# Projections from mixed token tiles, keys scaled on GpSimd, and a new spacing of the background steps beside a recurrent scan

## What is computed

```python
x = _layernorm(x + _L0_attn_ref(...))   # gated linear recurrence
x = _layernorm(x + _L0_xattn_ref(...))  # LSTM with attention in every step
x = _layernorm(x + _L0_ffn_ref(...))    # 8 experts, 2 a token: the FIRST mixture
x = _layernorm(x + _L1_attn_ref(...))   # the scan below
x = _layernorm(x + _L1_xattn_ref(...))  # cross attention
x = _layernorm(x + _L1_ffn_ref(...))    # 4 experts and a shared one: the SECOND mixture
```

```python
shifted = jnp.concatenate([zeros_like(h[:, :1]), h[:, :-1]], axis=1)
delta = shifted - h
xr = h + delta * x_r          # and xw, xk, xv, xa with x_w, x_k, x_v, x_a
r = xr @ W_r
log_w = -softplus(-(tanh(xw @ w_lora_a) @ w_lora_b + w_bias)) - 0.5
k = xk @ W_k
v = xv @ W_v
a = sigmoid(xa @ a_lora_a @ a_lora_b + a_bias)
g = sigmoid(r @ g_lora_a) @ g_lora_b + g_bias
kk = (k * k_k).reshape(Bn, Tn, H, D)
kk = kk / maximum(norm(kk, axis=-1, keepdims=True), 1e-12)
k = k * (1.0 + (a - 1.0) * k_a)
def step(S, xs):              # 512 steps, one after the other
    r_t, w_t, k_t, v_t, a_t, b_t = xs          # a = -kk, b = kk * a
    sa = einsum('bhij,bhj->bhi', S, a_t)
    S = S * exp(w_t)[:, :, None, :] + sa[..., None] * b_t[:, :, None, :] + v_t[..., None] * k_t[:, :, None, :]
    return S, einsum('bhij,bhj->bhi', S, r_t)
```

## Time and profile before

| | |
|---|---|
| time, median of 3 runs | 6065.13 us (6060.26 to 6067.42) |
| the profiled execution's own time | 6056.11 us |
| its span in the trace | 6054.3 us |
| busy in the span: PE, DVE, ACT, POOL | 5506.3, 3606.7, 2103.8, 317.7 us |
| mean granted TensorE clock | 0.973 of full speed |
| ahead of the tail phase's first scan step | 4342.3 us |
| the 512 scan steps | 4342.3 to 5785.6 us |
| what is left after them | 5785.6 to 6054.3 us |

### The profile page before, as it was taken

How to read it: one execution, slowest core, us unless ns; L and a number is a source line. 1 busy time by engine, 2 the same in 40 slices (tenths; PEclk the granted TensorE clock), 3 DMA queues, 4 the chain that set the end, 5 groups by cost and what they waited for, 6 DMA issues and landing times. The chain is left out here.

```text
span 6054.3 us, 385300 instructions
## 1 busy us (share of the span) xinstructions
PE 5506.3 (91%) x171736; PEld 3879.1 (64%) x171736; DVE 3606.7 (60%) x16290; ACT 2103.8 (35%) x8003; POOL 317.7 (5%) x779
## 2 busy tenths in 40 slices
PE   6899999999999999999999999999888879887989
PEld 2577777777777777777777777777644444444433
DVE  4355555555555555555555555555487898888831
ACT  3144444444444444444444444444222122223221
POOL 0000000000000000000000000000011111111000
PEclk8999999999999999999999999999899899899989
DMA  1100000000000000000000000000211101011111
GB/s 69 57 2 2 2 2 2 2 2 2 2 2 2 2 2 2 2 2 2 2 2 2 2 2 2 2 2 17 81 58 40 40 28 47 31 45 33 47 38 54
DMA packets 45135, 111.64 MB, mean 18 GB/s; under 512 B 8160, under 2 KB 10208, under 8 KB 44528
## 3 DMA queue, kind: packets, MB, share of 16 engines
q1 hardware_dynamic: 43600, 109.39, 5.6%
q10 hardware_dynamic: 1440, 1.06, 0.1%
HBM read 99.90 MB, written 10.52 MB: 18 GB/s over the span
## 5 line engine op out<-in xcount | busy, mean ns | idle before, releaser
L711 PE MATMUL lstm_part_ps<-lstm_keys,lstm_hid 128*4 128x128 f32 x32768 | 1024.1, 273 | 205.5 <-DVE lstm_hid L880 205.5
L727 PE MATMUL lstm_ctx_ps<-lstm_values,lstm_alpha 128*4 128x128 f32 (+1 forms) x49152 | 1051.4, 237 | 0.2 <-issue 0.2
L711 PEld LDWEIGHTS lstm_part_ps<-lstm_keys,lstm_hid 128*4 128x4 f32 x32768 | 771.3, 86 | 427.2 <-DVE lstm_hid L880 413.6
L727 PEld LDWEIGHTS lstm_ctx_ps<-lstm_values,lstm_alpha 128*4 128x4 f32 x49152 | 904.8, 86 | 90.7 <-issue 0.4
L909 DVE TENSOR_REDUCE lstm_neg_max<-lstm_part_ps 128x1 f32<-128x128 f32 x1024 | 299.1, 292 | 678.8 <-PE lstm_part_ps L711 678.8
L842 ACT ACTIVATE lstm_expo<-lstm_part_ps,lstm_neg_max 128x128 f32<-128x128 f32 x1024 | 376.4, 368 | 862.2 <-DVE lstm_neg_max L909 862.2
L670 PE MATMUL lstm_half_ps<-lstm_w_hid,lstm_hid 128*13 128x96 f32 x16384 | 596.0, 246 | 0.0
L862 DVE STREAM_TRANSPOSE lstm_gates<-lstm_half_ps 128x96 f32<-128x96 f32 x1026 | 290.1, 283 | 396.1 <-PE lstm_half_ps L670 372.0
L670 PE MATMUL lstm_half_ps<-lstm_w_attn,lstm_attn 128*13 128x96 f32 x16448 | 526.0, 248 | 0.0
L670 PEld LDWEIGHTS lstm_half_ps<-lstm_w_attn,lstm_attn 128*13 128x13 f32 x16448 | 300.5, 93 | 154.6 <-ACT lstm_attn L855 106.7
L1944 ACT ACTIVATE mix_gated<-mix_gate_ps 115x512 f32<-115x512 f32 (+2 forms) x200 | 112.6, 563 | 820.0 <-PE mix_gate_ps L1674 819.9
(11 more groups left out here) (336 smaller groups left out, 8593.0 us busy)
## 6 DMA issues: line engine op xcount, KB each, us to landing
mix_ring<-in_sm_chunks SPq DMA_DIRECT2D x120, 358.0 KB, 2.9
mix_ring<-in_mix_chunks SPq DMA_DIRECT2D x80, 384.0 KB, 3.0
lstm_xg<-xg_rows SPq DMA_DIRECT2D x514, 16.0 KB
xg_rows<-lstm_xg_tile SPq DMA_DIRECT2D x16, 512.0 KB, 2.6
ctxT<-in_ctxT SPq DMA_DIRECT2D x1, 2048.0 KB, 14.6
out_xT<-xT SPq DMA_DIRECT2D x4, 512.0 KB, 3.8
xT<-in_xT SPq DMA_DIRECT2D x1, 1536.0 KB, 9.8
lstm_w_x<-in_lstm_w_x SPq DMA_DIRECT2D x1, 1024.0 KB, 10.8
```

The lines of the kernel that those rows point to most:

```text
L711: mm = pe.matmul(part_rows(score_ps[part], b), hid[:, k, lo:lo + SPACE], keys[:, k, b * SRC + c * P:b * SRC + (c + 1) * P], start=(n == 0 ...
L727: mm = pe.matmul(part_rows(ctx_ps[n], b), alpha[:, b, c, SPACE - 1 - c:2 * SPACE - 1 - c], values[:, b * SC + c, ctx_cols[n]], start=(c == ...
```

## The change

Five things change, all in the tail phase.

1. The weights stay as they are loaded. For each tile GpSimd makes the difference of the two token tiles (`step_x`, 1 instruction, scan step 0), and VectorE makes five mixed tiles of it, one for each of r, w, k, v, a (`mix_x`, 10 SCALAR_TENSOR_TENSOR of 128x128, scan step 1). TensorE's `sums` has 2 products instead of 4. `project_columns` moves from step 0 to step 2 and waits for `mix_x`; ScalarE's `project_products` moves from step 1 to step 3.
2. The keys scaled by k_k are no longer a projection: ScalarE copies k, GpSimd multiplies it (`scale_keys`, step 5), and ScalarE squares that (`square_keys`, step 7).
3. `CHAIN_SLOTS = 1`: the hops of the norms and of the cross attention are 1 step apart instead of 2.
4. `CHUNK_SLOTS` is (3, 3) for the SECOND mixture; it stays (2, 3) for FIRST.
5. The weight preparation on VectorE ahead of the scan goes (16 instructions).

```diff
-CHUNK_SLOTS = (2, 3)
+CHAIN_SLOTS = 1
+CHUNK_SLOTS = {MIXTURE0: (2, 3), MIXTURE1: (3, 3)}
...
-                yield from attention(q, SLOTS)
+                yield from attention(q, CHAIN_SLOTS)
                 yield from mixture(SECOND, q, SLOTS)
...
-                for part in (OWN, LAST):
-                    for k in range(KC):
-                        mm = pe.matmul(out, lhs(part, k), rhs(part, k), start=(part == OWN and k == 0),
-                                       stop=(part == LAST and k == KC - 1))
+                for k in range(KC):
+                    mm = pe.matmul(out, lhs(k), rhs(k), start=(k == 0), stop=(k == KC - 1))
...
+            def mixed(name):
+                return lambda k: x_mix[:, MIXES.index(name), k, :]
...
             def project_columns(m):
-                pe.wait_ge(x_copied, m + 1)
+                pe.wait_ge(x_mixed, m + 1)
...
-                for n, name in enumerate(("k", "kk")):
-                    mm = sums(k_ps[:, n, :], x, lambda part, k: w[name][:, part, k, :])
-                mm.then_inc(keys_ready, 1)
+                sums(k_ps[:, 0, :], mixed("k"), lambda k: w["k"][:, k, :]).then_inc(keys_ready, 1)
...
-                if has_next and t == 0:
+                if has_next and t == 2:
                     project_columns(c + 1)
...
                 pe.wait_ge(added, added_by_mixture(x, i) + 1)
                 ln.mean(pe, lambda k: token_block(x, i)[:, k, :], g.mean_mat[:, :], width)
-                yield from pause(slots)
+                yield from pause(CHAIN_SLOTS)
                 ln.variance(pe, norm_after_mixture(x, i), g.mean_mat[:, :], width)
-                yield from pause(slots)
+                yield from pause(CHAIN_SLOTS)
                 ln.spread(pe, norm_after_mixture(x, i), g.spread, width)
-                yield from pause(slots)
+                yield from pause(CHAIN_SLOTS + 1)
...
             def keep_keys(m):
                 act.wait_ge(keys_ready, m + 1)
-                act.activation(kk_sq[:, :], k_ps[:, 1, :], ACT.Square).then_inc(kk_sq_ready, 1)
-                act.copy(k[:, :], k_ps[:, 0, :])
-                act.copy(kk[:, :], k_ps[:, 1, :]).then_inc(kk_ready, 1)
+                act.copy(k[:, :], k_ps[:, 0, :]).then_inc(k_copied, 1)
+
+            def square_keys(m):
+                act.wait_ge(kk_ready, m + 1)
+                act.activation(kk_sq[:, :], kk[:, :], ACT.Square).then_inc(kk_sq_ready, 1)
...
+            def step_x(m):
+                pool.wait_ge(x_copied, m + 1)
+                pool.tensor_tensor(x_step[:, :, :], x_in[:, LAST, :, :], x_in[:, OWN, :, :], ALU.subtract).then_inc(x_stepped, 1)
+
+            def scale_keys(m):
+                pool.wait_ge(k_copied, m + 1)
+                pool.tensor_tensor(kk[:, :], k[:, :], rows[:, K_K, :], ALU.mult).then_inc(kk_ready, 1)
...
+            def mix_x(m):
+
+                dve.wait_ge(x_stepped, m + 1)
+                for n in range(len(MIXES)):
+                    for k_ in range(KC):
+                        ins = dve.scalar_tensor_tensor(out=x_mix[:, n, k_, :], in0=x_step[:, k_, :], scalar=mix_w[:, n, k_:k_ + 1],
+                                                       in1=x_in[:, OWN, k_, :], op0=ALU.mult, op1=ALU.add)
+                ins.then_inc(x_mixed, 1)
...
+                if has_next and t == 1:
+                    mix_x(c + 1)
```

More of the change, by code:

```diff
@@ L1350, in decoder_tail_phase @@
         x_in = s.sb("rw_x_in", [P, 2, KC, P])
+        x_step = s.sb("rw_x_step", [P, KC, P])
+        x_mix = s.sb("rw_x_mix", [P, len(MIXES), KC, P])
         r_col = s.sb("rw_r_col", [P, KC, P])
@@ L1507, in pause, with chunk_slots @@
             return (None for _ in range(n))
-        def chunk_slots(n, slots, width):
-            return 1 if slots == 1 or width < NB else CHUNK_SLOTS[n % 2]
+        def chunk_slots(x, n, slots, width):
+            return 1 if slots == 1 or width < NB else CHUNK_SLOTS[x.x][n % 2]
         slot = {}
@@ L1731, in mixture @@
                         router[x].turn_weights(pe, i, ident[:, :], tiles)
-                    yield from pause(chunk_slots(n, slots, x.width(i)))
+                    yield from pause(chunk_slots(x, n, slots, x.width(i)))
                 down(count - 1)
@@ L1802, in attention @@
                 ln.spread(pe, norm_after_scan(q), g.spread, width)
-                yield from pause(slots)
+                yield from pause(slots + 1)
                 pe.wait_ge(ln_done, norm_after_scan(q) + 1)
@@ L1914, in scan_slot @@
                     copy_x(c + 1)
-                if has_next and t == 1:
+                if has_next and t == 3:
                     project_products(c + 1)
@@ L2087, in scan_slot @@
             def scan_slot(c, t, has_next, has_last):
+                if has_next and t == 0:
+                    step_x(c + 1)
+                if has_next and t == 5:
+                    scale_keys(c + 1)
                 if has_last and t == 10:
@@ L2277, in attention @@
                 ln.inverse(dve, norm_after_scan(q), width)
-                yield from pause(slots - 1)
+                yield from pause(slots)
                 ln.result(dve, norm_after_scan(q), block_x, width).then_inc(ln_done, 1)
@@ L2325, in _ @@
             beside = mixture(FIRST, 0, 1)
-            dve.tensor_scalar(less_k_a[:, :], rows[:, K_A, :], -1.0, 1.0, ALU.mult, ALU.add).then_inc(w_step, 1)
-            for _ in range(3):
-                next(beside, None)
-            for n, name in enumerate(MIXES):
-                of = w[name] if name in w else wa[name]
-                for k_ in range(KC):
-                    dve.tensor_scalar(of[:, LAST, k_, :], of[:, OWN, k_, :], mix_w[:, n, k_:k_ + 1], None, ALU.mult)\
-                       .then_inc(w_step, 1)
-                next(beside, None)
-                dve.wait_ge(w_step, 1 + KC * (n + 1))
-                dve.tensor_tensor(of[:, OWN, :, :], of[:, OWN, :, :], of[:, LAST, :, :], ALU.subtract).then_inc(w_own, 1)
-                next(beside, None)
-            dve.wait_ge(w_own, len(MIXES))
-            dve.tensor_tensor(w["kk"][:, :, :, :].rearrange("p a k n -> p (a k) n"), w["k"][:, :, :, :].rearrange("p a k n -> p (a k) n"),
-                              over_chunks(rows[:, K_K, :], 2 * KC), ALU.mult).then_inc(w_mixed, 1)
+            dve.tensor_scalar(less_k_a[:, :], rows[:, K_A, :], -1.0, 1.0, ALU.mult, ALU.add).then_inc(less_ready, 1)
             for _ in beside:
```

47 lines of the change are left out of this document (25 added, 22 removed).

## The result

The changed kernel takes 6051.98 us in the median (6047.19 to 6056.89, 20 runs), the kernel before, in the same job, 6063.13 (6057.87 to 6068.87, 20 runs): a ratio of 0.9982 with a 95% interval of 0.9975 to 0.9989, so 11 us less (7 to 15). It was forecast faster by 22. The profiled execution took 6052.22 us, its span is 6050.4, its granted clock 0.969 (0.973 before).

The account below looks back on a forecast made before the run. VectorE's time was taken to bound the scan steps: busy 1300.9, gaps 43.2 and waits 82 give 1426.1 us instead of 1443.3. With -3.7 ahead and -1 behind, -22 from 6065 gives 6043 us, range 6020 to 6053.

Parts of the forecast that it names:

- Busy time: VectorE in the scan steps: 1258.9 us before, plus 34.5 for mixing and 7.5 beside GpSimd, gives 1300.9.
- The GpSimd term: Scan steps: 30 new GpSimd instructions delay VectorE 0.25 us each, +7.5 us (bounds 0 and +15).
- Gaps: Scan steps: VectorE's small gaps between dependent instructions stay at 43.2 us.
- Projections: TensorE's projection line in the scan steps: 171.9 us falls by 100, to about 72.
- Mixtures: VectorE's waits in FIRST, SECOND and the router behind keys and values: from 129.1 to 36 us, -93.
- Hops: One step a hop in norms and attention: VectorE's waits there rise from 12.1 to 43 us, +31.
- Ahead and behind: Ahead of the scan, fewer first projections save 3.7 us; behind it, one step less gives -1.
- The wait for the difference: Mixed tiles in the scan: VectorE waits for GpSimd's difference, 3 us in all (bounds 0 and 30).
- Three steps a chunk: SECOND: waits for `up` nearly go, 9 us left; a tile takes about 80 us; no step is saved.
- The rival of the hops: Norms and attention wait 90 us instead of 43, deciding from 65: slower by 25 us, 6090; chance 0.13.
- The clock's rival: SECOND's chunks run at a lower TensorE clock, deciding below 0.85: slower by 43 us, 6108; chance 0.05.
- The pair of rows: 4561.95 and 4567.21: beside a GpSimd instruction `rw_kept` took 0.72 us instead of 0.28; priced at 0.25 each.

Follow-up runs that it names:

- mix_only: The changed kernel with the hops and chunks of before (two steps a hop, (2, 3) in both mixtures): 6032.14 us, -24.0 against before.
- pool_twice: mix_only with GpSimd's two new instructions of each tile done twice, the second time into spare buffers: 6042.40 us, -17.0 against before.
- shift2: mix_only with all chunks, norms and attention two steps later against the scan's own work: 6050.01 us, -9.4 against before.
- inverse2: The changed kernel with one more step between ScalarE's root and VectorE's inverse in every norm: 6070.90 us, +13.0 against before.

## Why the prediction was right, and where it was not

The sign and the range held, and most of the sum's terms did. The account of why it would be faster did not.

- *Busy time:* 1300.9 forecast, 1303.0 measured. The mixing takes 2.7 us a tile instead of 2.3 (40.6 instead of 34.5). The GpSimd term was 7.5; beside the mixing VectorE's busy time rose by 44.1 - 40.6 = 3.5. Doubling those instructions in mix_only cost 7 by the times and 11.6 by the busy time. So 0.25 an instruction was of the right size, and the runs tell it no better than 0.1 to 0.4.
- *Gaps:* 43.2 kept, 43.0 measured.
- *Projections:* line 1588 takes 87.7 us, not 72: a product of `rw_w_r` 21.7 / 120 = 0.18 us instead of 34.4 / 224 = 0.15. As TensorE is no longer the bound in SECOND, it cost little there.
- *Mixtures:* 36 us of waits forecast, 30.6 + 3.3 = 33.9 measured. The 3.3 of the router are not a gain in full, see `rw_kk_norm` below.
- *Hops:* 43 forecast (norms 23, attention 18, small rows 2), 53.7 measured (29.8, 20.5 and 3.4). The step that failed is the hop from root to inverse: 0.6 us a norm in the sum (11 x 0.6 = 7), 20.0 measured. The sum took it from the chain behind the scan, where ScalarE has nothing else. Beside the scan's work three roots stand behind the sigmoids of step 10 and two table loads, at 3.8 us each, and the other eight waited 1.1 on average.
- *`rw_kk_norm`:* 6.0, which no term had. It is no wait at a hop. It stands in the keys and values, where ScalarE's square root is queued behind a copy that waits for TensorE, and TensorE had waited for a transfer:

```profile
4580.15 3.39 PE L1756 MATMUL mix_gate_ps<-mix_gated,ca_w_k 128*128 128x512 f32 x4 [5.02 <-DMA mix_gated<-in_ctxT]
4588.75 1.01 ACT L1974 COPY ca_values<-mix_down_ps 128x1024 f32<-128x1024 f32 x1 [2.77 <-PE mix_down_ps L1762]
4589.91 0.25 DVE L2165 RECIPROCAL rw_kk_norm<-rw_kk_norm 128x16 f32<-128x16 f32 x1 [6.05 <-ACT rw_kk_norm L1891]
```

Before, TensorE waited 5.8 us for the same transfer, and VectorE then waited once behind the keys and values, 9.6 us at the router. That wait is 1.7 now, so most of what the router lost seems to have moved here; no run tests it.
- *Ahead and behind:* -3.7 forecast, -2.6 measured; -1 forecast, -3.2 measured. The wait for the difference, 3, was 0.

So the scan steps came to 1439.6 instead of 1426.1, by these terms: +2.1 busy, -2.1 in the mixtures, +10.7 in norms and attention, +6.0 for `rw_kk_norm`, -3 for the difference. With 1.1 more ahead of the scan and 2.2 less behind it that is some 12 us, the miss of 22 against 11.

The larger error stands under **Three steps a chunk**. The mixtures' fall of 93 us was one term for three edits, and I set the hops' +31 against all of it. mix_only shows 63 of it to come from the mixed tiles alone (129.1 to 65.8). The spacing gave only the last 32 and brought 51 of others (8.2 to 59.7, `rw_kk_norm` with it); by the two differences to before, -24 and -11, the kernel got some 13 us slower by it. Before the change TensorE was 10 us a tile over VectorE in SECOND, and once the first edit had taken that away, the second had little left to win. The forecast was right in the whole and blind to the fact that half of the change works against it. That its total held is in part luck, since a gain from the mixed tiles and a loss from the spacing met inside its range. The rival of the hops named the mechanism: 4 us a norm with TensorE at the half clock and ScalarE's projections between. The trace shows 3.8 in three norms with the projections between, and the waits at the hops stayed under its 65.

The clock's rival did not come: 0.92 in a SECOND tile, where it was to decide below 0.85. Its "88 to 97% busy" misreads the rows, where TensorE is busy 96 and 97% of the two tiles. The pair of rows priced VectorE's delay beside GpSimd about right: 0.23 us of time, or 0.39 of busy time, for each of 30 instructions in pool_twice. By the strict rule that the prediction took from the Trainium skill (SBUF — State Buffer, Who interferes with whom), that the two engines exclude each other for a whole instruction, it priced each at 0.62; that would have been up to 18 us of busy time, where 11.6 came.

What stays open: what in a position decides most of the waits. The root on step 10 is one such overlap, seen in both kernels; it gives 4.0 of the 14.6 us that two steps cost in shift2, and the rest is not told apart; and inverse2's 23.5 us of other waits may be its own shift or the longer chain. By this one trial, a forecast of such a reordering from sums of busy time should carry some 15 us either way for place alone.

## What to carry to other kernels

Where a change has several edits against the same wait, price each on what the others leave: a wait is taken away once. A chain of hops between engines must be timed with what its engines have in their queues in that very step, their table loads too, and not from a stretch where they are free. And when one engine's time bounds the loop, look for an idle one to take the work, with a step more between the two than seems needed.

## What the hardware showed beyond the forecast

- ScalarE's table loads took 1.28 us each, and the order alone changed how many there are: with the same work, `silu` loaded its table 32 times in mix_only and 41 times in the changed kernel. The other lines gave some back, so that all loads together are 115 and 121. Of a switch the Trainium skill (ScalarE: Activation LUTs, What ACT_TABLE_LOAD costs) says 1.28 us of loading and a drain of 1.38 beside it. The rows of 4566.69 and 4567.98 show the load alone: it began 0.02 us after the instruction before it ended (4565.61 + 1.06), and the sigmoid followed 0.01 us after it. So these switches cost 1.28 us each, and no drain shows.

```profile
L1946 ACT ACT_TABLE_LOAD x41 | 52.6, 1283 | 0.7
```

- One VectorE addition of 1280 columns took 1.48 us, ten SCALAR_TENSOR_TENSOR of 128 columns 2.7 us. ScalarE took 0.39 us for each of its ten products of 128 columns.
- GpSimd's subtraction of 128x256 took 1.20 us in the mean, but 0.75 in the median, with single ones up to 2.57; the one in the earlier trace rows, of the same size, took 0.62. No run here shows what the long ones met.
